# Selective-scan convolution layer: logarithm, positive part and first variance product moved to the tiles behind a group's first

## The reference

```python
xz = x @ in_proj_w.T + in_proj_b
xin, z = jnp.split(xz, 2, axis=-1)                 # 192 channels each
xc = silu(depthwise_conv3x3(xin) + conv_b)
u = xc.reshape(b, D_INNER, L)                      # L = 1024
x_dbl = jnp.einsum('bdl,kd->blk', u, x_proj_w)
dt, Bv, Cv = jnp.split(x_dbl, [DT_RANK, DT_RANK + D_STATE], axis=-1)
dt = jnp.einsum('blr,dr->bdl', dt, dt_proj_w)
A = -jnp.exp(A_log)
delta = jax.nn.softplus(dt + dt_proj_b[None, :, None])
# for each position: h = exp(delta * A) * h + delta * u * B;  y = sum_n h * C
y = scan(...) + u * Ds[None, :, None]
mu = y.mean(-1, keepdims=True)
var = y.var(-1, keepdims=True)
y = (y - mu) * jax.lax.rsqrt(var + 1e-05) * ln_g + ln_b
y = y * jax.nn.silu(z)
return y @ out_proj_w.T + out_proj_b
```

## Time and profile before

| what | value |
|---|---|
| median of 3 runs | 3813.66 us (3811.82 to 3817.78) |
| profiled execution: time, span | 3815.76 us, 3813.9 us |
| TensorE matmul busy | 2849.4 us (75%) |
| VectorE busy | 3266.3 us (86%) |
| ScalarE busy | 2051.3 us (54%) |
| GpSimd busy | 2350.1 us (62%) |
| granted TensorE clock, mean | 0.779 |

### The profile page before, as it was taken

One profiled execution on the slowest core, in us unless ns is written; L12 is line 12 of the kernel. 1 busy time (PEld: TensorE's weight loads), 2 busy tenths in 40 slices (PEclk: granted clock), 3 DMA queues, 4 the chain that ended last, 5 costly groups with the idle time before them and its releaser, 6 DMA issues. The chain is left out here.

```text
span 3813.9 us, 26717 instructions
## 1 busy us (share of the span) xinstructions
PE 2849.4 (75%) x6084; PEld 648.1 (17%) x6084; DVE 3266.3 (86%) x2104; ACT 2051.3 (54%) x2278; POOL 2350.1 (62%) x1004
## 2 busy tenths in 40 slices
PE   6778777877887788435667677688778887887887
PEld 2111111111111211111111121111111111111111
DVE  1899999999999998585988924999999999999993
ACT  3465555656565655314555425556565556656562
POOL 1677767777776776003656504677676767776773
PEclk9677787878788877767789777677887778788778
DMA  2555546463655554103443405365546555564742
GB/s 57 136 126 139 138 125 143 119 161 97 160 129 133 124 133 117 28 0 84 117 106 85 99 5 122 99 160 133 129 115 142 135 128 126 132 153 109 157 119 62
DMA packets 140377, 436.95 MB, mean 115 GB/s; under 512 B 33429, under 2 KB 34139, under 8 KB 139915
## 3 DMA queue, kind: packets, MB, share of 16 engines
q1 hardware_dynamic: 140234, 435.53, 47.4%
HBM read 307.50 MB, written 6.82 MB: 82 GB/s over the span
## 5 line engine op out<-in xcount | busy, mean ns | idle before, releaser
L841 POOL TENSOR_TENSOR L_read<-L_state,L_c_rows 128x1024 f32<-128x1024 f32 x768 | 1809.0, 2362 | 757.1 <-DVE L_state L931 467.3
L931 DVE TENSOR_TENSOR_SCAN L_state<-L_decay,L_b_ps 128x1024 f32<-128x1024 f32 x768 | 1756.0, 2286 | 29.4 <-DVE L_b_ps L916 2.1
L651 PE MATMUL L_y_ps<-L_read,L_fold 128*64 128x512 f32 x3072 | 1255.0, 913 | 394.8 <-POOL L_read L841 375.5
L916 DVE TENSOR_TENSOR L_b_ps<-L_du,L_b_ps 128x1024 f32<-128x1024 f32 x768 | 937.5, 1221 | 236.0 <-issue 146.4
L777 ACT ACTIVATE L_decay<-L_delta,L_a_neg 128x1024 f32<-128x1024 f32 x768 | 876.4, 1145 | 406.7 <-DVE L_state L931 405.7
L767 ACT COPY L_b_ps<-L_b_rows 128x1024 f32<-128x1024 f32 x256 | 260.1, 1016 | 340.6 <-DVE L_state L931 220.6
L651 PEld LDWEIGHTS L_y_ps<-L_read,L_fold 128*64 128x64 f32 x3072 | 188.0, 161 | 1356.5 <-POOL L_read L841 1017.6
L1461 POOL TENSOR_TENSOR L_read<-L_state,L_c_rows 128x1024 f32<-128x1024 f32 x96 | 237.3, 2477 | 184.3 <-PE L_y_ps L1257 109.5
L1567 DVE TENSOR_TENSOR_SCAN L_state<-L_decay,L_b_ps 128x1024 f32<-128x1024 f32 x96 | 219.5, 2286 | 3.3
L626 PE MATMUL L_side_ps<-L_dbl,L_w_dt 128*128 128x512 f32 x216 | 182.4, 940 | 50.3 <-DVE L_sq_b L902 26.9
L626 PE MATMUL L_side_ps<-g_cm,L_w_u 96*128 (+1 forms) x216 | 179.7, 921 | 41.7 <-ACT L_u L695 40.0
(11 more groups left out here) (315 smaller groups left out, 2677.3 us busy)
## 6 DMA issues: line engine op xcount, KB each, us to landing
L_c_rows<-L_bc_dram SPq DMA_DIRECT2D x580, 256.0 KB, 4.0
L_b_rows<-L_bc_dram SPq DMA_DIRECT2D x580, 256.0 KB, 4.2
L_delta<-L_delta SPq DMA_DIRECT2D x204, 256.0 KB, 5.8
L_du<-L_du SPq DMA_DIRECT2D x140, 256.0 KB, 5.8
L_du<-L_u SPq DMA_DIRECT2D x64, 256.0 KB, 6.1
L_bc_dram<-L_dbl SPq DMA_DIRECT2D x40, 128.0 KB, 3.4
L_delta<-L_delta_a SPq DMA_DIRECT2D x16, 256.0 KB, 4.4
L_du<-L_du_a SPq DMA_DIRECT2D x16, 256.0 KB, 5.5
```

The source lines that it names most:

```text
L651: m = nc.tensor.matmul(y_ps[i * BLK:(i + 1) * BLK, c, :], fold[:, :], y_half(t, o, i), start=first, stop=last, skip_group_check=True)
L841: nc.gpsimd.tensor_tensor(read[:, t % READS, :], state[:, t % STATES, :], c_rows[:, g % 2, :], ALU.mult).then_inc(multiplied, 1)
L916: nc.vector.tensor_tensor(to[:, :], du2[:, d * NBLK + c, :], row[:, :], ALU.mult).then_inc(injected, 1)
L931: nc.vector.tensor_tensor_scan(state[:, t % STATES, way], decay[:, t % DECAYS, way], fed[:, way], 0.0, ALU.mult, ALU.add).then_inc(scanned, 1)
```

## The change

Five table entries of L2 are rewritten; nothing is added or removed, and the other layers keep their order.

```diff
-               ("var", 0): (17, 18), ("out", 0): (19, 20)}
+               ("var", 0): (18, 18), ("out", 0): (19, 20)}
...
-CONV_ACT = {14: (("exp", 0),), 15: (("log", 0),), 16: (("one", 0), ("less", 0)), 17: (("exp", 1), ("log", 1)),
-            18: (("one", 1), ("less", 1), ("relu", 0)), 19: (("relu", 1),)}
+CONV_ACT = {14: (("exp", 0),), 16: (("log", 0), ("one", 0)), 17: (("less", 0), ("exp", 1), ("log", 1)),
+            19: (("relu", 0), ("one", 1), ("less", 1)), 20: (("relu", 1),)}
...
-CONV_POOL = {14: ("gap", 0), 16: ("gap", 1), 18: ("du", 0), 19: ("du", 1)}
+CONV_POOL = {15: ("gap", 0), 17: ("gap", 1), 18: ("du", 0), 20: ("du", 1)}
```

## The result

The changed kernel takes 3820.38 us (median of 8 runs, 3815.52 to 3826.99), the kernel before 3810.94 us (8 runs in the same session, 3807.25 to 3817.78): a ratio of 1.0025, 95% interval 1.0014 to 1.0036, so some 5 to 14 us slower. That is inside the range and 1.3 us above the predicted time. So close a hit is in part luck: the prediction started from 3813.66 us, and the kernel before measured 2.7 us less here, so the difference is +9.4 us where +5.4 was forecast. The ratio lies just beyond the 0.2% that the prediction counted as no change, with an interval on both sides of it; no change was given most of the chance, although the prediction's own sum pointed to slower.

What follows compares the result with a forecast made beforehand. Turn ends were taken as bound by POOL's multiplication 20, then SP and DMA; turn 3 by VectorE, without slack. Terms 1.7 + 0.3 + 0.3 + 3.1 = +5.4 us on 3813.66 gave 3819.1; range 3810 to 3823.

Steps and rivals of the forecast that it cites:

- no change: Whole kernel: a time within 0.2%, 7.6 us, of before; chance 0.76.
- Two chains at the end of turns 0 to 2: VectorE's queue and POOL multiplication 20 to SP to DMA; the second ends last, by about 1 us (4.24 in turn 0).
- The paying stall: Rival, turns 1 and 2: VectorE's queue sets their ends, each gains 2.3 us; total -3.3 us, 3810.4; chance 0.13.
- VectorE wins 2.3 us at tile 21 and waits that much longer at the next tile 0: Ends of turns 1 and 2: B row copied 2.9 us earlier, less 0.6; the gain returns as waiting.
- in the regained slack: Turns 1 and 2: VectorE's first output product comes 0.7 us later, covered by the time won at tile 21.
- Turns 1 and 2, +0.3 each: Fold 18 comes 0.7 us later, so POOL's multiplication 20 starts at 1972.1 instead of 1971.82: +0.3 us per turn.
- the first sum's 0.3 us: Turns 1 and 2: TensorE's first sum waits for the positive part, 1954.3 instead of 1954.03.
- Turn 0, +1.7: First sum waits for the positive part: +0.3 us after POOL's relief, +1.4 from TensorE's low clock; bounds 0.3 to 3.3.
- Turn 3, +3.1: Output product later by 1.05 us at unchanged clock; +3.1 with TensorE at 1.2 GHz for 4.3 us after idling.
- the row of 8.5 us: Turn 3 profile row: TensorE's low level from 2155.88 to about 2164.4 after 4.10 us idling; as bound, +5.0.
- The tail, 0: Last scan's start to the next layer's first statistics; the forecast sum holds no term for it.
- the lasting low clock: Rival, turn 0's first sums and turn 3's second variance product: slow clock lasts; +8.9 us, 3822.6; chance 0.21.

Runs made afterwards that it cites:

- SP's new order: Kernel before, and change with turn 3's variance product put back, each loading C after B's rows and block 1's copies: 3804.47 and 3808.8 us.
- the variance move alone: Kernel before with only the first variance product moved from tile 17 to 18, in all turns and the tail: ratio 1.0012.
- six matmuls: Changed kernel plus six matmuls of zeros between the two variance products of turn 3: ratio 1.0016 to the kernel before.
- the softplus moves alone: Changed kernel with the first variance product put back to tile 17, so only ScalarE and POOL steps move: ratio 1.0001 to the kernel before.
- four matmuls: Changed kernel plus four matmuls of zeros between the two variance products of turn 3: ratio 1.0018 to the kernel before.

## Why the prediction was right, and where not

**Two chains at the end of turns 0 to 2: right.** From SP's load of C, right behind multiplication 20, to tile 2 it is 15.8 to 17.8 us at the thirty ends of turns 0 to 2 in the ten executions with SP's old order (16.3 to 16.6 in the one predicted from), and in the one that moves only the variance product the shorter stall is worth -0.2 to +0.2 us. The paying stall is refuted there; the same kernels with SP's new order, which differ in more than the stall, show no gain from it either. That multiplication 20 carries the turn shows in the changed kernel's turn 1: it came 2.9 us later, and the turn took 3.0 us more.

**"VectorE wins 2.3 us at tile 21 and waits that much longer at the next tile 0": half right.** It waits longer, but at the output product (1.00 to 4.11), not at tile 0 (1.12 to 0.69). The prediction had put that product's 0.7 us "in the regained slack" without noting that VectorE already waited 1.00 us for it. The sum did not depend on it. A slip in the same passage: 2.85 + 1.0 + 2.1 + 0.75 + 2.1 is 8.8 and not 8.9; the trace of the changed kernel has 8.91 us from the third sum to fold 18 (1964.63 to 1973.54), so the 0.1 us stood, by luck.

**Turns 1 and 2, +0.3 each: too small.** Where the first sum kept its clock the turn took 117.8 us on average (eight turns, in both executions of the change and four experiments with its softplus order), against 117.0 for the six turns of before and of the variance move alone: +0.8. In four of twelve turns the first sum ran at 1.2 GHz and the turn took 120.0 us on average: +3.0. Together +1.5 us a turn. The mis-sized term is the first sum's 0.3 us: its wait was costed, its clock was not. In turn 1 of the profiled execution its low clock alone put the second sum 5.31 instead of 3.58 us behind it, +1.7.

**Turn 0, +1.7: +1.1 measured** (mean of six, 111.0, against 109.9 of three). The mechanism was as told, the rise came some 3.5 us after the new start (1839.41; the third pair takes 1.02), where 4.3 was taken.

**Turn 3, +3.1: +4.3 and +3.5 measured** (89.90 and 89.06 against 85.56, the execution of before in which, as in both of the change, the clock was up again before the centring was done; against the other execution of before, 89.31, there is almost none, +0.6 and -0.3. The seven executions with the old order in this turn took 84.4 to 89.3 us, 85.9 on average). Order and place were right (idle 4.31 us for a forecast of 4.2). What failed is "I take +3.1", the low level for 4.3 us: it lasted 7.7 and 7.3 us, nearer the row of 8.5 us that had been kept as the bound because six of seven others were shorter. The nearest row in kind, the other gap of 4 us in the same turn, was the better guide, though not a firm one: in the second execution of before that row has some 19 us.

**The tail, 0: open.** It took 58.4 to 58.7 us in three executions (both of the change, and six matmuls) and 55.7 to 57.0 in the other nine. TensorE stands at 1.2 GHz in all of their tails, and only how long differs (to 2235 in the changed kernel, 2222 before). Turn 3's idling does not explain it: the variance move alone has that idling and a tail of 55.8 us, and six matmuls filled it and left a tail of 58.4 us. Whether the change adds to it is not settled.

Sum of the means: 1.1 + 3.0 + 3.9 = +8.0 us without the tail, +10 with it (+8.4 if both executions of before are averaged in every place); the medians say +9.4 (5 to 14). The direction and the places were right, the size was 4 us short: the first sums' clock in turns 1 and 2, at nothing in the prediction, and the length of the low level in turn 3. Of the rivals, the lasting low clock (+8.9) came nearest: true in turn 3, not in turn 0, and with a share in turns 1 and 2 that no case had.

## What to carry to other kernels

Before a stall is shortened, look for the next wait on the same engine, also one of 1 us: here two chains stood behind it, and 6 us of stall were worth nothing. A product moved so that TensorE idles for several us can cost more by the clock than by its order (here 3.6 against 1.05 us). A load that waits at the head of a queue delays all behind it, and reordering it was the one cheap gain here.

## What was not expected of the hardware

- Behind the same idling TensorE's low level does not last the same time. In turn 3 of the same program it took 8.5 us in one execution and about 19 in the other, with TensorE busy without a pause. A single profiled execution gives such a price only to within some 4 us.
- With 1.82 us of idling in front of the first sum, the low level was there in four of eleven turns; with 1.59 to 1.60 us in none of the six turns of before and of the variance move alone. The same program showed it in turn 1 in one execution and in turn 2 in the next. The idling just ahead of the sum is not the whole cause: in the three turns of the softplus order with 1.44 us there (turn 2 of the softplus moves alone, turn 1 with four matmuls, turn 2 of the change with SP's new order), the level had fallen 7 us ahead of the sum and was back before it. So it fell in 7 of 14 such turns, and what decides was not isolated.
- SP's issues are not of one length: the same load of C's rows took 1.10 us behind the wait for multiplication 20 (1977.22) and 2.50 us right behind the copies of block 1 (1972.72). What makes it longer was not isolated; it may be part of why the new order gave less in turn 0 than the move suggested.
